# Attention and gated feed-forward on one core: the next batch's input, values, first keys and queries made inside the last steps of the batch before

## The reference

```
xn = layernorm(x)                                    # x: 4 x 1024 x 1024
q, k, v = xn @ Wq.T, xn @ Wk.T, xn @ Wv.T            # 16 query heads, 4 key/value heads, size 64
att = softmax(mask(q @ k.T / 8))                     # causal, last 512 keys and the first 4 (the sink)
s = (att @ v) @ Wo.T                                 # query head h reads key/value head h // 4
x_norm  = layer_norm(xn) * in_gamma + in_beta
thought = x_norm[:, -1, :] @ agg_w + agg_b           # one row per sequence
for _ in range(4):
    t = gelu(layer_norm(thought, pn) @ d1_w + d1_b)  # width 4096
    thought = thought + t @ d2_w + d2_b
out = layer_norm(xn + sigmoid(xn @ gate_w + gate_b) * (thought @ bc_w + bc_b))
result = x + s * silu(out)
```

## Time and profile before

| | |
|---|---|
| median of 3 runs | 2451.33 us (2449.65 to 2454.17) |
| profiled execution | 2447.99 us, span 2446.3 us |
| mean granted TensorE clock | 0.956 of full speed |
| PE busy | 2248.7 us, 92% of the span |
| first scores; last values product done | 176.8 us; 1677.6 us |
| batches' steps begin at | 176.8, 577.5, 976.4, 1375.7 us |

### The profile page before, as it was taken

How to read it: one execution, slowest core, us unless ns; L and a number is a source line. 1 busy time by engine, 2 the same in 40 slices (tenths; PEclk the granted TensorE clock), 3 DMA queues, 4 the chain that set the end, 5 groups by cost and what they waited for, 6 DMA issues and landing times. The chain is left out here.

```text
span 2446.3 us, 35525 instructions
## 1 busy us (share of the span) xinstructions
PE 2248.7 (92%) x13576; PEld 1655.2 (68%) x13576; DVE 1496.4 (61%) x3084; ACT 884.4 (36%) x1842; POOL 143.6 (6%) x352
## 2 busy tenths in 40 slices
PE   3779999779999969999987999996899999999998
PEld 2556666567666647666656666663688888888887
DVE  3536666665666654666665566663576666766666
ACT  2215555523555532555552355552311111111111
POOL 1100000010000011000001000000011010111000
PEclk6889999999999989999998999997799999999999
DMA  8664444564334454454355534433634433344331
GB/s 311 240 189 166 156 162 139 179 178 158 133 127 168 171 179 140 169 168 146 132 195 162 174 126 143 168 135 120 230 126 137 137 118 112 130 137 129 131 116 63
DMA packets 164667, 379.08 MB, mean 155 GB/s; under 512 B 18648, under 2 KB 100632, under 8 KB 148656
## 3 DMA queue, kind: packets, MB, share of 16 engines
q1 hardware_dynamic: 157680, 354.06, 42.9%
q0 software_dynamic: 5120, 16.85, 1.9%
q10 hardware_dynamic: 1728, 6.29, 0.7%
HBM read 297.37 MB, written 79.72 MB: 154 GB/s over the span
## 5 line engine op out<-in xcount | busy, mean ns | idle before, releaser
L591 ACT ACTIVATE pt<-t_ps 128x512 f32<-128x512 f32 x480 | 266.5, 596 | 496.3 <-PE t_ps L788 493.4
L988 DVE CUSTOM_DVE_ANT_0 probs<-s_ps,mask 128x644 f32<-128x644 f32 (+5 forms) x512 | 317.2, 656 | 95.6 <-PE s_ps L761 92.7
L600 ACT ACTIVATE probs<-probs,neg_max 128x644 f32<-128x644 f32 (+5 forms) x512 | 352.9, 694 | 21.2 <-DVE neg_max L988 21.2
L710 PE MATMUL j_ps<-x_hi,w 128*128 128x512 f32 x960 | 320.4, 405 | 16.0 <-DMA w<-WT 16.0
L788 PE MATMUL t_ps<-ident,probs 128*128 128x128 f32 x1920 | 273.9, 282 | 7.2 <-ACT pt L591 4.2
L1332 PE MATMUL out_ps<-wo,by_hi 128*128 128x512 f32 x1024 | 273.7, 389 | 0.0
L761 PEld LDWEIGHTS s_ps<-k_hi,q 64*128 64x128 f32 x1536 | 145.4, 184 | 170.2 <-DVE neg_max L988 77.1
L761 PE MATMUL s_ps<-k_hi,q 64*128 64x512 f32 (+4 forms) x1536 | 242.1, 351 | 4.2 <-DVE neg_max L988 4.2
L788 PEld LDWEIGHTS t_ps<-ident,probs 128*128 128x128 f32 x1920 | 212.0, 142 | 48.6 <-issue 15.5
L812 PE MATMUL o_ps<-pt,v 128*64 128x256 f32 x1920 | 235.5, 386 | 0.0
L1005 DVE TENSOR_SCALAR probs<-probs,inv_sum 128x644 f32<-128x644 f32 (+5 forms) x512 | 217.9, 468 | 9.1
(11 more groups left out here) (153 smaller groups left out, 2973.2 us busy)
## 6 DMA issues: line engine op xcount, KB each, us to landing
fw<-in_L_ffn_d_w_dram SPq DMA_DIRECT2D x128, 1024.0 KB, 5.0
w<-WT SPq DMA_DIRECT2D x40, 1024.0 KB, 5.1
probs<-in_L_attn_x_dram POOLq DMA_DIRECT2D x32, 512.0 KB, 5.6
XS<-x_hi SPq DMA_DIRECT2D x32, 512.0 KB, 4.4
XS<-x_lo SPq DMA_DIRECT2D x32, 512.0 KB, 6.2
Y<-y SPq DMA_DIRECT2D x128, 128.0 KB, 1.8
b_x<-in_L_attn_x_dram SPq DMA_DIRECT2D x32, 512.0 KB, 4.2
b_y<-Y SPq DMA_DIRECT2D x32, 512.0 KB, 6.4
```

The source lines that it names most:

```text
L591: act.activation(pt[:, m % PT_SLOTS, :, :], bank[:, :].rearrange("p (h q) -> p h q", q=P), ACT.Copy).then_inc(pt_ready, 1)
L600: act.activation(probs[:, slot, 0:width], probs[:, slot, 0:width], ACT.Exp, bias=neg_max[:, slot:slot + 1], scale=-1.0, accum_out=row_sum[ ...
L710: last = pe.matmul(out[:, :], weights[:, wp * C + c * P:wp * C + c * P + P], xs[:, c, bass.ts(ch, BANK)], start=i == 0, stop=i == STEPS - 1)
L988: dve.tensor_tensor_reduce(out=probs[:, slot, 0:width], in0=s_ps[head % 2][:, 0:width], in1=m, scale=-SCALE, scalar=-NEG, op0=ALU.add, op1 ...
```

## The change

The front stage of the batches 1 to 3 is gone as a stage. What it made is spread over the steps of the batch before:

- Every step has up to four *places* on PE (`places`, `fill`): 0 behind the first transposes, 1 behind the second, 2 behind the third, 3 behind the values product. Steps 23 to 30 make the next batch's block `t = s - 23`: its first four transposes in place 0, the other four in place 1. Steps 27 to 30 also make two blocks of values, in the places 2 and 3. Step 26 makes a key piece in place 2; step 31 makes the second key piece and the first two query pieces in the places 0, 1 and 2.
- All of these go through the one bank `j_ps`, in one numbered order (`ORDER`, `NUMBER`): a piece starts when the one before it has been taken (`j_taken`). Only ahead of the first step of batch 0 do seven banks take turns.
- ACT and DVE take a piece at fixed positions of their own step (`take_place`). DVE also has the statistics of the next block behind its masks of heads 2 and 3, and its norm near the end of the step.
- Heads are set up anew: a pair of query heads comes from two key/value groups (`head_of`), so a key piece is copied once, with two key heads in the two halves of the partitions; batches need two key pieces ahead of the steps, and the other two are made in the steps 7 and 11. Values have three sets of buffers.
- Query pieces are spread otherwise: step 4, 8, 20, 24 and 25 hold a whole piece, 24 and 25 in place 2 alone; the last batch has no piece in the steps 23 and 26 to 31. The feed-forward's tiles lie in the steps 2 to 17 and 19 to 31, two tiles in 22, 23 and 26.
- The sum of the last round, the fold and the new `thought` are made in the steps 0 and 1 of the next batch.
- SP's queue loads the first query weights ahead of the stores of x; the keys' weights have a third slot of `w`.
- To serve the new order of heads, `prepare_weights` loads each tile in two DMAs of 64 rows, and `finish` loads each of the eight Wo tiles in two DMAs that write runs of 64 elements (256 bytes).

```
-        FILL = ((0, 14), (14, STEPS), (0, 14), (14, STEPS))
-        def piece_at(s):
-            half, part = divmod(s, 4)
-            piece = 2 * half + 2 + part // 2
-            return (piece, *FILL[part]) if piece < 4 * KV else None
+        for t, s in enumerate((19, 20, 21, 22, 22, 23, 23, 24, 25, 26, 26, 27, 28, 29, 30, 31)):
+            TILES_AT[s].append(D1_TILES + t)
+        QUERIES = {0: (2, 0, 14), 1: (2, 14, STEPS), 2: (3, 0, 14), 3: (3, 14, STEPS),
+                   4: (4, 0, STEPS), 5: (5, 0, 14), 6: (5, 14, STEPS),
+                   8: (6, 0, STEPS), 9: (7, 0, 14), 10: (7, 14, STEPS),
+                   20: (12, 0, STEPS), 21: (13, 0, 12), 22: (13, 12, STEPS), 24: (14, 0, STEPS), 25: (15, 0, STEPS)}
+        KEYS = {7: 2, 11: 3}
+        TURN0 = 23
+        def places(b, s):
+            found = [None] * 4
...
+            if b + 1 < B:
+                t = s - TURN0
+                if 0 <= t < TB:
+                    found[0], found[1] = ("x", b + 1, 2 * t, 0, STEPS), ("x", b + 1, 2 * t + 1, 0, STEPS)
+                if 4 <= t < TB:
+                    found[2], found[3] = ("v", b + 1, 2 * t - 8, 0, STEPS), ("v", b + 1, 2 * t - 7, 0, STEPS)
+                if t == 3:
+                    found[2] = ("k", b + 1, 0, 0, STEPS)
+                if s == UNITS - 1:
+                    found[0] = ("k", b + 1, 1, 0, STEPS)
+                    found[1], found[2] = ("q", b + 1, 0, 0, STEPS), ("q", b + 1, 1, 0, STEPS)
+            return found
...
+                def wait_bank(made):
+                    n = NUMBER[made]
+                    if n >= EARLY:
+                        pe.wait_ge(j_taken, n)
...
                 def step(b, s):                                   # PE
                     scores(b, s, 0)
                     turn_two(0)
+                    fill(0)
                     ffn_step(b, s)
                     scores(b, s, 1)
                     turn_two(2)
-                    if fill:
-                        piece, a, z = fill
-                        q_proj(b, piece, a, (a + z) // 2)
+                    fill(1)
                     turn_two(4)
-                    if fill:
-                        q_proj(b, piece, (a + z) // 2, z)
-                    if s:
-                        values(b, s - 1)
+                    fill(2)
+                    if u:
+                        values(u - 1)
+                    fill(3)
...
+                    for i in range(min(n, 2)):                    # ACT
+                        take_turned(u - 1, i)
+                    exponentials(b, s, 0)
+                    exponentials(b, s, 1)
+                    take_place(0)
+                    for i in range(2, min(n, 4)):
+                        take_turned(u - 1, i)
+                    exponentials(b, s, 2)
+                    take_place(1)
...
                     mask_scores(b, s, 0)                          # DVE
+                    mask_scores(b, s, 1)
+                    take_place(0)
                     if TILES_AT[s]:
                         add_sums(b, s)
                     mask_scores(b, s, 2)
                     mask_scores(b, s, 3)
+                    if ahead is not None:
+                        stats(b + 1, ahead)
                     invert(b, s, 0)
                     divide(b, s, 0)
                     divide(b, s, 1)
+                    take_place(1)
...
+                    else:                                         # finish, Wo
+                        for half in range(2):
+                            sp.dma_start(raw[n % RAW][:, :].rearrange("p (m r h d) -> p h m r d", m=2, r=4, h=2)[:, half],
+                                         Wo[bass.ts(n // 2, P), :].rearrange("p (m h r d) -> p h m r d", m=2, h=2, r=4
+                                                                             )[:, half]).then_inc(raw_loaded[n % RAW], 16)
```

## The result

Median 2469.45 us (2469.25 to 2469.67, four runs) beside 2450.49 us for the kernel before on the same chip: ratio 1.0081, 95% interval 1.0063 to 1.0098. The changed kernel is 0.8% slower. The forecast was 2470.

What follows compares the result with a forecast made beforehand. PE bounds the steps; batch borders idle, with 31.6 us each to hide. Start -20, three borders +28, last batch +3, `prepare_weights` +0.5 and Wo +12 gave +23.5 on 2448.0: 2471.5, stated as 2470 us, range 2392 to 2500.

Steps and rivals of the forecast that it cites:

- The mechanism and the place: Steps 25 to 29 of three batches: PE waits 4 to 5 us for `j_ps`, released by DVE's `x_lo`.
- the clock: Borders: seven long PE waits each followed by half-speed matmuls, charged 1.5 us each, 10.5 us a border.
- The waits of a border: Steps 24 to 31: PE waits for takers sum to 33.3 us a border; forecast branch 28 to 40, 52%.
- The start: Ahead of batch 0's steps: 16.0 us weights wait gone, about 4 from key copies and first query piece; -20 us.
- The last batch: Seven steps without a piece, four before, each idling some 0.75 us against the softmax chain: +3 us.
- Wo: `finish`: eight Wo tiles loaded in runs of 256 bytes, +12 us, the middle of +5 and +20.
- The lower bound: Wo loads in `finish`: runs of 256 bytes move no less a byte, 1.85 us a tile, +5 us for eight.
- The upper bound: Wo loads in `finish`: a 256-byte run costs as much as one of 512, 3.7 us a tile, +20 us.
- The handshake half as bad: Rival, 18%: ACT and DVE reach their places earlier, waits of 17 us a border, few drops; 2390 to 2420 us.
- It comes out even: Rival, 12%: waits of 25 us a border, drops for half, -4 us a border, start pays for Wo; 2440 to 2455.
- PE fed throughout: Rival, 12%: everything at the borders hidden, x's second half taken within 1 us of its transposes; -100 us, 2350 us.
- A late load: Rival, 6%: x's block lands after the next step's masks, DVE stands some 5 us a step; +100, above 2500 us.

Runs made afterwards that it cites:

- run 1: Changed kernel with DVE's statistics of the next block of x moved to the very start of the step: 2440.4 us (ratio 0.9959 to the kernel before).
- run 2: Changed kernel with DVE's subtraction of x's second half moved ahead of the first reciprocal and two divisions: 2447.4 us (0.9988 to the kernel before).
- run 5: Changed kernel with only ACT's two copies of x moved ahead of its exponentials, DVE's order unchanged: 2439.6 us (0.9950 to the kernel before).
- run 4: Changed kernel with DVE's statistics and second subtraction and ACT's two copies of x all moved earlier: 2389.0 us (0.9754 to the kernel before).
- run 6: Kernel before, with SP's queue loading the first query weights ahead of the sixteen stores of x: 2434.9 us (0.9936).
- run 7: Changed kernel with each Wo tile loaded by one DMA of whole rows, heads paired wrongly, a price only: 2464.5 us (1.0059 to the kernel before).
- run 9: run 4 with PE's values products of the step before put ahead of place 2 in steps with x: 2392.7 us (0.9775 to the kernel before).
- run 12: run 4 with statistics directly behind the taking of x's second half, and Wo in whole rows reordered by PE: 2379.1 us (0.9708 to the kernel before).
- run 3: Changed kernel with both DVE edits, statistics at the step's start and second subtraction ahead of the divisions: 2437.1 us (0.9946 to the kernel before).
- run 8: Changed kernel with Wo loaded in whole rows and its heads ordered by sixteen PE products a tile: 2464.6 us (1.0065 to the kernel before).

## Why the prediction was right, point by point

**The mechanism and the place** were as written: in-order takers, place 2, released by DVE's `x_lo`, and the clock behind it. Step 28's subtraction was due to end at +11.6 and ended at +11.1; the wait was to be 5.1 and was 4.66. Runs 1, 2 and 5 each shorten one link of the chain and each shorten the longest wait, 4.7 us, to 3.2, 3.6 and 3.9. Run 4, which shortens three, has 1.5. So the chain is shown, not argued. The signs came too, the sizes a little smaller: first scores at 147.9 us for 146, the marks of step 1 on average 408 us apart for 409, 3.5 to 4.7 us at place 2 in steps 25 to 29 for 4 to 5, and the first gate product 7.8 us later behind the last values product for 12.

**The waits of a border were sized too high, the clock too low.** Forecast 33.3 us; the waits of steps 24 to 31 of batch 0 are 27.8: 2.5, 4.4, 3.9, 4.7, 4.7, 4.2, 2.6 and 0.9. Those of steps 24 to 29 are 0.4 to 0.9 us below their forecasts, and the 1.9 for step 24's first transposes didn't come. A wait of 1.8 for the sinks stood in step 23, which I hadn't listed. The clock was to cost 10.5 and cost 12.6 by the stretch rows. With the measured sizes -31.6 + 29.6 + 12.6 - 3.0 gives +7.6 a border; the marks give +9.1, the forecast +9.2. No cause was found for the 1.5 us between 7.6 and 9.1.

**The start** was 3 us too good: -16.9. The 16.0 of the wait was right within 1.2 (run 6). Of the 4 us for fewer key copies and a warm first piece about 2 are left, and the traces' spread ahead of that mark, 152.5 to 158.3 us, is larger than that; no run tests them by themselves.

**The last batch** cost +4.6 for +3. By the view by stretch PE idles 4.7 us between its marks for 2.9 before, so the unfilled steps cost 1.8. The other 2.8 are busy time, at a granted clock of 0.99 for 1.00; run 5, at 1.00, has the same stretch in 308.7 us for 310.4, so 1.6 of it are clock.

**Wo** was the worst term: +12, the middle of 5 to 20, where run 7 shows 5.0 us in the medians and 0.74 a tile, 6 for eight, in the traces. The lower bound, a byte costs what it costs, was the right reading: 0.6 a tile. The error was to take the middle between ends far apart on the price of runs of 512 bytes, which were stores to HBM and not loads. The stage as a whole cost +7.8: another 1.9 us lie ahead of its first tile, 41.1 us from the last values product for 39.2, and run 7 has them as well, so they aren't Wo's. What they are wasn't found. The Trainium skill, *DMA: Bandwidth & Descriptors*, section "Why small descriptors are slow (HBM only)", with 11 cycles for 8, came to +4 by estimate; the 5 to 6 us measured are more than that. The upper bound asked 2.45 us more a tile, and no run here shows such a price on these loads. I had taken the same page of the Trainium skill, section "Specifications", on read-modify-write under 512 bytes, as speaking for it.

**The sum.** In the profiled executions +21.7 us stand for a forecast of +23.5: Wo's runs were 6 too dear and the end 1 shorter, while start and last batch together were 5 too cheap and the 1.9 us ahead of Wo were missing. That the sum is so close is luck. That the border's term is close is half luck, since its two parts erred by 4 and 2 us against each other and 1.5 us are not explained. The number itself had more luck: 2470 was the sum on a profiled 2448.0, rounded down, and the same sum on the median of 2451.3 would have been 2474.8. Between the medians the change cost 19.0 us.

**The rivals.** The handshake half as bad would have needed 17 us a border; run 4 has 9 for `x_lo` and some 14 with the waits for y, masks and sinks, and is in effect the kernel that this rival described, at 2389 for its 2390 to 2420. What it lacked is what I had held against it: the order on DVE and ACT. It comes out even had 25 us of waits a border, and the 27.8 measured for its list lie nearer to that than to the 33.3 of the forecast and just below its branch of 28 to 40. What sets this rival's -4 us a border apart from the +9.1 measured is mainly the clock, 12.6 us for its 6, then the waits, 29.6 with the sinks for its 25. PE fed throughout stays untried: one j_ps bank leaves about 1.4 us for each hand-off (copy 0.60, subtraction 0.69), and run 9 only moved it. A late load didn't come: DVE's statistics wait for no load of x in the changed kernel between 360 and 1400 us.

## What to carry to other kernels

Before moving work into the gaps of a busy engine, lay out one step on the engines that take its results, instruction by instruction: with a single bank the producer waits for the taker's position in its own queue, not for its speed. Then move the taking: here four calls moved (the statistics, DVE's second subtraction, ACT's two copies) turned +0.8% into -2.5%, and no work changed. Waits of PE cost their length and, when they are long or many enough, the clock as well, so the last ones removed can bring more than the first. And removing one wait can lengthen another: run 12 took out 13 us of waits and lost most of it again to 4.5 us at another place and the clock behind them.

## What the runs showed of the hardware

- Seven waits of 0.9 to 1.5 us and five of up to 0.5, in the steps 24 to 30, left the granted clock at 1.00 over 111 us (run 4, batch 0); with seven waits of 2.5 to 4.7 us it was 0.89 (changed kernel). It isn't the sum alone: run 5 idles 20.1 us in its stretch at a clock of 0.88, run 3 19.8 us at 0.95. The longest wait for `x_lo` there is 3.6 us in the one and 2.8 in the other.
- Nor is it the length of a single wait. Ahead of step 24 of batch 0, run 4 has one of 1.99 us and the granted clock is 1.00 from 392 to 400 us; run 12 has one of 1.98 and 0.61 from 393 to 400:

```profile
391.97 1.06 PE L764 MATMUL o_ps<-fw,cols 128*32 128x512 f32 x8 [1.99 <-DVE y L1118]
```

```profile
391.52 1.01 PE L921 MATMUL o_ps<-small_rows 16*64 16x256 f32 x4 [1.98 <-DVE small_rows L1128]
```

- Loads from HBM that write runs of 256 bytes: 0.74 us more for 512 KB than whole rows. This is in a stretch bound by DMA: from 1730 to 1760 us in the changed kernel its share is 1.12 at 294 GB/s, and in the same stage of run 7, from 1734 to 1759, 0.95 at 360 GB/s.
- Sixteen products of 64 columns with the identity bring 128 rows into another order of heads as they are transposed, and cost at most 0.6 us here, where PE waits for a DMA (774.2 us for 773.6 from the last values product to the end, runs 8 and 7).
